# Three full passes and two pairs of half-width products for a 3x3 convolution on one core

## What is computed

```python
x = x + routed_convolution(group_norm(x))     # first stage
x = x + mamba_rows_then_columns(group_norm(x))  # second stage
```

```python
k, v = x @ Wk, x @ Wv                     # 2 heads of 16
attn = softmax over pixels of (q . k / 4)
logits = (sum over pixels of attn * v) @ Wmlp     # 4 experts
w = top-2 of softmax(masked logits / 1.5), rescaled
x_mod = x * (1 + mean over heads of attn * 1024 * softplus(alpha))
y = sum over e of w[e] * (conv3x3(x_mod, We[e]) + be[e])
```

## Time and profile before

| | before |
|---|---|
| median of 3 runs | 3953.78 us (3950.43 to 3957.21) |
| the profiled execution | 3949.65 us, its span 3947.8 us |
| granted clock over the span | 0.993 |
| busy shares of the span | PE 93%, VectorE 95%, ScalarE 74%, GpSimd 83% |

### The profile page before, as it was taken

How to read it: one execution, slowest core, us unless ns; L and a number is a source line. 1 busy time by engine, 2 the same in 40 slices (tenths; PEclk the granted TensorE clock), 3 DMA queues, 4 the chain that set the end, 5 groups by cost and what they waited for, 6 DMA issues and landing times. The chain is left out here.

```text
span 3947.8 us, 34409 instructions
## 1 busy us (share of the span) xinstructions
PE 3654.2 (93%) x8780; PEld 1519.6 (38%) x8780; DVE 3749.1 (95%) x3409; ACT 2937.3 (74%) x4422; POOL 3277.5 (83%) x1542
## 2 busy tenths in 40 slices
PE   7999999899999999999999999999999999999998
PEld 3444444333333333333333333333333333333333
DVE  7778787999999999999999999999999999999998
ACT  3454554787888878888888888878888888878785
POOL 2221222899999999999999999999999999999998
PEclk9999999999999999999999999999999999999999
DMA  4142324888888888898888888888899888988886
GB/s 113 33 130 58 109 74 149 325 344 338 347 348 348 344 345 340 345 350 353 347 342 350 347 347 342 352 347 341 343 353 349 339 346 347 350 340 344 336 348 264
DMA packets 203157, 1181.06 MB, mean 299 GB/s; under 512 B 30960, under 2 KB 31760, under 8 KB 68816
## 3 DMA queue, kind: packets, MB, share of 16 engines
q1 hardware_dynamic: 200128, 1177.64, 77.5%
q10 hardware_dynamic: 2832, 1.23, 0.1%
HBM read 1144.03 MB, written 34.73 MB: 299 GB/s over the span
## 5 line engine op out<-in xcount | busy, mean ns | idle before, releaser
L1537 POOL TENSOR_TENSOR read<-state,bc_all 128x1024 f32<-128x1024 f32 x1024 | 2398.9, 2360 | 117.0 <-DVE state L1601 88.0
L1601 DVE TENSOR_TENSOR_SCAN state<-decays,p_drive 128x1024 f32<-128x1024 f32 x1024 | 2297.9, 2274 | 33.0 <-ACT p_drive L1436 9.8
L1306 PE MATMUL p_y<-read,ident 128*128 128x512 f32 x4096 | 1921.9, 602 | 14.0 <-POOL read L1537 13.9
L1428 ACT ACTIVATE decays<-dt,wa 128x496 f32<-128x496 f32 x2048 | 1337.2, 703 | 121.1 <-DVE state L1601 118.5
L1306 PEld LDWEIGHTS p_y<-read,ident 128*128 128x128 f32 x4096 | 764.9, 191 | 990.6 <-issue 833.2
L1588 DVE TENSOR_TENSOR p_drive<-bc_all,p_dtx 128x1024 f32<-128x1024 f32 x768 | 906.5, 1210 | 0.0
L1554 POOL TENSOR_TENSOR pool_drive<-dtx,bc_all 128x1024 f32<-128x1024 f32 x256 | 602.4, 2353 | 12.2 <-DMA bc_all<-bc_scratch 11.9
L766 POOL TENSOR_TENSOR pad<-map_all,xc 128x512 f32<-128x512 f32 x96 | 138.9, 1476 | 519.1 <-DMA map_all<-map_scratch 498.3
L1436 ACT COPY p_drive<-pool_drive 128x1024 f32<-128x1024 f32 x256 | 260.8, 1019 | 270.8 <-DVE state L1601 270.8
L1302 PE MATMUL p_y<-xconv,d_diag 128*128 128x512 f32 x256 | 144.6, 647 | 202.0 <-DVE gated L1611 202.0
L556 PE MATMUL p_conv<-pad,wm 128*128 128x512 f32 x576 | 267.5, 600 | 1.8 <-issue 1.8
(11 more groups left out here) (162 smaller groups left out, 3214.1 us busy)
## 6 DMA issues: line engine op xcount, KB each, us to landing
bc_all<-bc_scratch SPq DMA_DIRECT2D x1024, 1024.0 KB, 7.3
map_all<-map_scratch SPq DMA_DIRECT2D x48, 512.0 KB, 5.7
norm_rows<-xn SPq DMA_DIRECT2D x32, 280.0 KB, 5.8
norm_in<-norm_rows SPq DMA_DIRECT2D x64, 140.0 KB, 6.6
norm_in<-norm_rows SPq DMA_DIRECT2D x64, 139.8 KB, 7.6
fresh<-in_x SPq DMA_DIRECT2D x32, 256.0 KB, 6.8
x<-in_x SPq DMA_DIRECT2D x32, 256.0 KB, 3.6
mid_x<-x SPq DMA_DIRECT2D x32, 256.0 KB, 6.5
```

The costliest lines, as they stand in the source:

```text
L1306: nc.tensor.matmul(p_y[:], ident[:], read[:, s % DEEP, :], start=False, stop=(s == N - 1)).then_inc(y_added, 1)
L1428: nc.scalar.activation(decays[:, s % DEEP, :].rearrange("p (q t) -> p q t", t=SIDE)[:, :, 1:], dt[b][:, :, 1:], ACT.Exp, scale=wa[m][:, s: ...
L1537: nc.gpsimd.tensor_tensor(read[:, s % DEEP:s % DEEP + 2, :], state[:, s % DEEP:s % DEEP + 2, :], bc_all[s // CHUNK][:, :, 1, :], ALU.mult) ...
L1601: nc.vector.tensor_tensor_scan(state[:, at:at + 2, :].rearrange("p s n -> p (s n)"), decays[:, at:at + 2, :].rearrange("p s n -> p (s n)") ...
```

## The change

The convolution keeps the three main products. The three full-size other products become two pairs of products of 64 output columns. One of a pair writes PSUM partitions 0 to 63 from a tile `above`, the other 64 to 127 from a tile `below`. So that two pairs do for three column offsets, each tile holds the rows needed twice: one half of its partitions as they are, and the other half moved by one column. This takes 4 copies of ScalarE for an image where there were 2. The tiles are one for each image of a team, no longer one for each team too. The mixed weights shrink from 768 to 640 columns. Scores and values become four products of 32 output columns each, for the four images side by side in `p_route` and in a bank of their own, `p_value`; all eight are issued in one place. The results lie on 128 partitions in place of 64. The copies are spread over ScalarE's slot. Group normalization takes its PSUM from `p_modul`. In stage 2, five chunks of `bc_all` are loaded early in place of seven, and two wait for the last convolution.

```diff
@@ conv_main, conv_anti
         for dx in range(3):
-            nc.tensor.matmul(bank[:], w_mixed[g][a][:, 0, dx, :], padded[g][a][:, :, dx:dx + SIDE],
+            nc.tensor.matmul(bank[:], w_mixed[g][a][:, 128 * dx:128 * dx + 128], padded[g][a][:, :, dx:dx + SIDE],
                              start=(dx == 0), stop=False)
...
-        for dx in range(3):
-            mm = nc.tensor.matmul(bank[:], w_mixed[g][a][:, 1, dx, :], shifted[g][a][:, :, dx:dx + SIDE],
-                                  start=False, stop=(dx == 2))
+        for n, dx in enumerate((0, 2)):
+            at = MAIN + 128 * n
+            nc.tensor.matmul(bank[0:64, :], w_mixed[g][a][:, at:at + 64], above_rows[a][:, :, dx:dx + SIDE],
+                             start=False, stop=(n == 1))
+            mm = nc.tensor.matmul(bank[64:128, :], w_mixed[g][a][:, at + 64:at + 128], below_rows[a][:, :, dx:dx + SIDE],
+                                  start=False, stop=(n == 1))
         mm.then_inc(conv_done, 1)
@@ scores
-            mm = nc.tensor.matmul(p_route[:], route[:, 128 * a:128 * a + 128], xc[g][a][:], start=(a == 0), stop=(a == TEAM - 1))
-            if a == TEAM - 1:
-                mm.then_inc(score_done, 1)
+            for a in team:
+                if t:
+                    pe.wait_ge(x_step, 16 * i + (4 * (k - 2) + a + 1))
+                nc.tensor.matmul(p_route[32 * a:32 * a + 32, :], route[:, 0, :], xc[g][a][:], start=True, stop=True)
+            for a in team:
+                mm = nc.tensor.matmul(p_value[32 * a:32 * a + 32, :], route[:, 1, :], xc[g][a][:], start=True, stop=True)
+            mm.then_inc(score_done, 1)
@@ TensorE's slot
             if runs_conv:
                 conv_main(pe, *last, 0)
-            score(i, k, TEAM - 1)
+            scores(i, k)
             if runs_conv:
                 conv_anti(pe, *last, 0)
...
-            if after:
-                for a in range(TEAM - 1):
-                    score(*((i, k + 1) if k < PHASES - 1 else (i + 1, 0)), a)
@@ shift
-        ge(act, conv_done, 4 * (P - 2) + a + 1)
-        act.wait_ge(padded_ready, 4 * P + a + 1)
-        nc.scalar.copy(shifted[g][a][0:64, 0:ROWS2 - 1, :], padded[g][a][0:64, 1:, :])
-        nc.scalar.copy(shifted[g][a][64:128, 1:ROWS2, :],
-                       padded[g][a][64:128, :ROWS2 - 1, :]).then_inc(shifted_ready, 1)
+        if pieces[0] == 0:
+            ge(act, conv_done, 4 * (P - 1) + a + 1)
+            act.wait_ge(padded_ready, 4 * P + a + 1)
+        src, up, down = padded[g][a], above_rows[a], below_rows[a]
+        if 0 in pieces:
+            nc.scalar.copy(up[64:128, 1:, :], src[64:128, :ROWS2 - 1, :])
+        if 1 in pieces:
+            nc.scalar.copy(up[0:64, 1:, 0:SIDE + 1], src[64:128, :ROWS2 - 1, 1:])
+        if 2 in pieces:
+            nc.scalar.copy(down[0:64, :ROWS2 - 1, :], src[0:64, 1:, :])
+        if 3 in pieces:
+            nc.scalar.copy(down[64:128, :ROWS2 - 1, 0:SIDE + 1], src[0:64, 1:, 1:]).then_inc(shifted_ready, 1)
@@ ScalarE's slot
+            if P:
+                shift(act, P - 1, 1 - g, 1, (1, 2, 3))
             if steps:
                 step_out(i, k - 1, 0)
+            if P:
+                shift(act, P - 1, 1 - g, 2, range(4))
             if norm:
                 group_root(act, norm[0])
+            if P:
+                shift(act, P - 1, 1 - g, 3, (0, 1))
             act.wait_ge(wexp_in, P + 1)
...
+            if P:
+                shift(act, P - 1, 1 - g, 3, (2, 3))
             act.wait_ge(wsel_ready, P + 1)
...
-            shift(act, P, g, 0)
-            shift(act, P, g, 1)
-            if after:
-                shift(act, P, g, 2)
-                shift(act, P, g, 3)
+            shift(act, P, g, 0, range(4))
+            shift(act, P, g, 1, (0,) if after else range(4))
@@ stage 2, spread_first and spread_rest
-        sp.wait_ge(s1["w_ready"], 96)
-        for k in range(CHUNKS - 1):
+        for k in range(FREE_EARLY):
             spread_chunk(sp, 0, k)
...
+        sp.wait_ge(s1["conv_done"], 96)
+        for k in range(FREE_EARLY, CHUNKS - 1):
+            spread_chunk(sp, 0, k)
```

More of the change, by code:

```diff
@@ L46, in build @@
         both_par = sb("both_par", [128, 128])
[L47 to L49 removed]
+        pick = sb("pick", [128, 4, EXPERTS])
+        spread = sb("spread", [128, 128])
+        route = sb("route", [128, 2, 32])
         ones = sb("ones", [128, 128])
@@ L104, in build @@
         dve_chain = sem("dve_chain")
[L106 to L107 removed]
         first_loads = [(wk_sb[:], wk), (q_sb[:], q.partition_broadcast(128)), (wv_sb[:], wvT), (wmlp_sb[:], wmlp),
                        (gain[:, 0:1], alpha.partition_broadcast(128))]
+        BOTH, ONE = MAIN + 128, MAIN + 192
         expert_loads = [(be_sb[:], be), (we_sb[:, :, 0:MAIN], we[:, :, 0:MAIN])]
[L112 to L115 removed]
+        for rows, moves in ((slice(0, 64), ((MAIN, 192), (MAIN + 64, MAIN), (ONE, BOTH))),
+                            (slice(64, 128), ((MAIN, MAIN), (MAIN + 64, 128), (BOTH, BOTH)))):
+            for to, source in moves:
+                expert_loads.append((we_sb[rows, :, to:to + 64], we[rows, :, source:source + 64]))
         mamba_loads = []
@@ L229, in _ @@
             for off in (0, 4):
-                place(pick[:], 1.0, -off, [[-16, 4], [-1, EXPERTS]], n + 1)
-                place(spread[:].rearrange("p (r h a) -> p r h a", r=16, h=2), 1.0, -off, [[0, 16], [-8, 2], [-16, 4]], n + 2)
+                place(pick[:], 1.0, -off, [[-32, 4], [-1, EXPERTS]], n + 1)
+                place(spread[:].rearrange("p (r h a) -> p r h a", r=16, h=2), 1.0, -off, [[0, 16], [-8, 2], [-32, 4]], n + 2)
                 n += 2
@@ L245, in _ @@
             nc.vector.memset(route[:], 0.0).then_inc(dve_chain, 1)
-            for e in range(EXPERTS):
-                for par in range(2):
-                    nc.vector.memset(anti_of(slice(64 * par, 64 * par + 64), par, e), 0.0)
+            nc.vector.memset(we_sb[0:64, :, BOTH:ONE], 0.0)
+            nc.vector.memset(we_sb[64:128, :, ONE:], 0.0)
             s1["norm_first"](dve)
@@ L530, in sync_program, with p_gn, group_mean @@
         each_phase(sp, slot)
-    def group_mean(pe, n):
+    def p_gn(n):
+        return p_small if n >= 4 * BODIES - 2 else p_modul
+    def group_mean(pe, n, maps=0):
         pe.wait_ge(gn_mean_in, n + 1)
-        nc.tensor.matmul(p_gn[:, P_MEAN], c["group_mean"][:], moments[:, :, 0],
+        ge(pe, map_ready, maps)
+        nc.tensor.matmul(p_gn(n)[:, P_MEAN], c["group_mean"][:], moments[:, :, 0],
                          start=True, stop=True).then_inc(gn_mean, 1)
@@ L653, in tensor_program @@
         pe.wait_ge(c["route_ready"], 1)
-        for a in range(TEAM - 1):
-            score(0, 0, a)
         pe.wait_ge(c["const_built"], 10)
-        pe.wait_ge(zeroed, ZEROS)
-        pe.wait_ge(zeroed_dve, ZEROS_DVE)
         each_phase(pe, slot)
@@ L1059, in stage2 @@
         early[k] for k in ("norm_in", "xconv", "soft", "relu", "dt", "dtx", "bc_rows"))
-    bc_all = [sb(f"bc_all{k}", [128, CHUNK, 2, PIX]) for k in range(CHUNKS - 1)]
+    FREE_EARLY = 5
+    bc_all = [sb(f"bc_all{k}", [128, CHUNK, 2, PIX]) for k in range(FREE_EARLY)]
     pool_drive = [sb(f"pool_drive{b}", [128, 2, PIX]) for b in two]
     decays = sb("decays", [128, DEEP, PIX])
+    bc_all += [sb(f"bc_all{k}", [128, CHUNK, 2, PIX]) for k in range(FREE_EARLY, CHUNKS - 1)]
     state = sb("state", [128, DEEP, PIX])
@@ L1534, in read_states @@
             pool.wait_ge(scan_done, PAIRS * u + s // 2 + 1)
-            if u == 0 and s == DEEP - 2:
+            if u == 0 and s == 4:
                 pool.wait_ge(s1["stored"][0], STORED)
```

96 lines of the change are left out of this document (42 added, 54 removed).

## The result

The changed kernel takes 3967.3 us (median of 12 runs, 3960.9 to 3974.6) against 3954.4 for the kernel before, run beside it (12 runs). The ratio is 1.0035, with a 95% interval of 1.0026 to 1.0044: 0.35% slower, which is small but clear of the scatter.

The account below looks back on a forecast made before the run. TensorE bound 17 of 23 phase intervals, VectorE six; afterwards the loop over the map bounds the 17. Terms -17.3 (intervals), +25.6 (clock falls) and +2 (ends) give +10.3 on 3953.8: 3964 us, range 3934 to 3992.

Parts of the forecast that it names:

- So column tiles run side by side: TensorE: products to different output columns overlap, so an image's two pairs take 1.72 us in place of 2.57.
- rival B: TensorE: column tiles overlap only in part, 3971 to 3995 us; chance 0.16.
- C: TensorE: column tiles don't overlap at all, 34.0 us for a phase, 4121 in all; chance 0.04.
- 22.0 us: TensorE's own work in a phase after the change, down from 26.07.
- done at 8.6: ScalarE's chain: the map ends 8.6 us after neg_top began, before 8.7.
- ScalarE is late, not VectorE: Ahead of the logits' exponential: nine copies and an output step free ScalarE after the logits, ready some 0.6 us earlier than 7.3.
- 25.7: Loop over the map: period in us of the 17 intervals not bound by VectorE, without a change of clock.
- 26.8: The six VectorE-bound intervals, in us, down from 28.2 through weight passes 640 wide in place of 768.
- 3.7 us in each phase: TensorE's idle time before main 0, from a loop of 25.7 less its own work of 22.0.
- between 0 and 1.7, and I take 1.4: Cost in us of one fall of TensorE's clock after the pause; 23.8 over 17 intervals, 1.8 over the six.
- The ends, taken as +2: Before the first neg_top and from the last into stage 2: no large term, between -3 and +6 us.
- Rival A: TensorE's clock stays up despite the pause before main 0: -17.3 + 2, giving 3938.5 us; chance 0.26.

Follow-up runs that it names:

- experiment 8: Changed kernel with three constant products in TensorE's pause, two of image 3's copies moved behind the map, and scores' semaphore and swap earlier: 3925.1 us.
- experiments 2 and 3: Changed kernel each time: first, two of image 3's copies moved behind the map, 3941.7 us; second, two copies an image instead of four, 3946.3 us.
- experiment 1: Changed kernel with three full float32 products of constants as filler behind each phase's last convolution product, in TensorE's pause: 3936.0 us, ratio 0.9955.
- experiment 5: Changed kernel with each image's four 64-column products replaced by three full-size ones, TensorE's old amount of convolution: 3948.1 us, ratio 0.9984.

## Why the prediction came out right, step by step

**TensorE's new work.** "So column tiles run side by side" held, and the scores that had no row came near the lower bound: 1.85 us for sixteen records where 1.7 was put. The eight records of 64 columns of an image start in pairs, 0.43 to 0.48 apart. The rule of the Trainium skill on the row group, by which the sum would have stood near rival B, doesn't show here: the loads of 64 columns, 0.13 to 0.14 us each, don't slow this pace. The same section of the Trainium skill (TensorE: Matmul & The Clock Gate, Part 3, The mechanism) also lets a load for the background weight buffer go ahead of running matmuls, which the prediction left out. Rivals B and C are out by these rows. "22.0 us" for a phase held: in experiment 8, where TensorE has no pause, 24.52 - 2.57 = 21.95. In the changed kernel a phase less the pause and the fall is 27.45 - 3.40 - 1.7 = 22.4, since small waits lie inside it, such as 0.17 for a copy of ScalarE ahead of anti 1.

**The second loop.** Map "done at 8.6": 8.57 in the ordinary phases without normalization. "ScalarE is late, not VectorE": no idle time ahead of L735; experiments 2 and 3 show by how much, 0.6 us, and that the rest of the copies is covered. With the clock held up (experiment 1) the ordinary intervals average the "25.7" of the sum, and two errors cancel in this. From the fetch to `pad` "7.5" was phase 9's own value; the mean of the ordinary phases is 7.2, before and after, so those without normalization take 25.6. And the six of the 16 with normalization, which the sum mentions but gives no term, have the map at 9.04 and take 26.0. The terms as written add up to 25.7, not to the 25.8 given. The six VectorE-bound intervals, "26.8": 26.6.

**The clock.** A gap of "3.7 us in each phase": 3.0 to 3.9, 3.4 on the mean of the ordinary ones. "The lower level after nearly each": after 21 of 22. The cost of a fall was put too low: "between 0 and 1.7, and I take 1.4" was 1.7, the upper end, since the slow records begin about when work resumes and next to nothing of the fall lies in the idle time.

**The sum.** For the 23 intervals the prediction has 597.7 + 25.6 = 623.3; they take 632.9. Of these 9.6 us the first interval has 3.6 (30.7 for 27.1), the ordinary ones 16 x 0.3 = 4.8, the six 6 x 0.2 = 1.2. In these six the fall costs 0.7 where 0.3 was put, but their base is 0.2 lower. The ends, taken as +2, are -3.2 + 2.8 = -0.4. Together that is the 7.2 between +10.3 and the +17.5 of the profiled executions. Between the medians the distance is 2.6 only: the profiled execution of the kernel before is 4.7 below its median of now, that of the changed kernel at its own. So the mechanism came as forecast, and that the forecast of 3964 lies 3 us from the median is better than its terms were.

**The ends.** "I see no large term" failed for the first interval, 30.7 instead of 27.0. Before, three score products ran while the first `pad` was awaited; now none is left for that time, TensorE is idle for 11.62 us, and main 0 takes 5.39 us and the scores 2.08, 2.9 more than with the clock up. The filler kernel, which has no products in that first pause either, keeps 29.8. The first `neg_top` comes 3.2 us sooner, which no term foresaw and which happens to take this back. The last 2.8 us lie behind the last `neg_top`; among all kernels run here, whose stage 2 is the same but for its first loads, this rest of the span varies from 3303 to 3315 us, so they can't be told from scatter.

**The rivals.** Rival A, the clock staying up, is what the filler kernel makes true: A was put 15.3 us under the kernel before, and filler's median is 15.6 under the one beside it. The agreement is in part luck, since its 23 intervals take 14.1 less where A had 17.3. The changed kernel itself is not A, since the gap, named as the evidence against A, came nearly as computed.

## What to carry to other kernels

Before an engine's work is cut, the loop that stands next under it wants measuring: here it had 0.8 us of room, so that the 4 us saved on TensorE in a phase bought a pause, and the pause lowered the clock for the very products on that loop. The saving is real once the order lets it be used: the same products, with the next scores taken into the pause, were 0.8% faster than the kernel before, and 1.0% with the first two phases of a body served apart. A delay put in on purpose tells the room of a loop, and also shows collisions that end when something comes later.

## What the runs showed of the hardware

- Column tiles of float32 products run side by side, four of 32 columns too (16 records in 1.85 us), and records of one half pass earlier ones of the other: L574's first started with three records of L570 still ahead of it in the program.
- Of 22 pauses of 3.0 to 3.9 us in TensorE 21 were followed by a stretch at 1.2 GHz; of 22 pauses of 1.2 to 1.9 us (experiment 5) two were: 0.93 against 0.99 over 500 us. Where the pauses were 2.3 to 3.0 us (experiment 2) 7 of 22 phases escaped, and an ordinary interval fell by 1.3 us for 0.6 us of loop.
- The fall begins about when work resumes (294.20 for both), so its cost, 1.7 us, lies on the work behind the pause.
- GpSimd's `pad` and VectorE's passes over the weights slow each other: two passes of 768 columns took 1.94 us apart from it, 3.97 beside it, and 2.97 when it began 0.85 later than they did; `pad` itself took 4.95 us apart and 6.87 beside them. With the map 1.53 us later, the six intervals were 1.06 us shorter on the mean.
